# Layer 1's cosine sums: both layer norms of the tokens as one scale, ln_g and ln_b in ScalarE's evictions, a Gram matrix of unscaled queries, unrolled batches

## What is computed

```
x = x + _L1_xattn_ref(_layernorm(x, axis=-1), ctx_1024, ctx_1024, ...)

def layer_norm(x, g, b, eps=1e-05):
    mu = x.mean(-1, keepdims=True)
    var = ((x - mu) ** 2).mean(-1, keepdims=True)
    return (x - mu) / jnp.sqrt(var + eps) * g + b

f_q, f_k, f_v = (proj(q), proj(k), proj(v))      # proj: layer_norm(t, ln_g, ln_b) @ w_in.T
q_centered = f_q - f_q.mean(-1, keepdims=True)
feat_corr = jnp.einsum('hnd,hne->hde', q_flat, q_flat) / q_flat.shape[1]
q_global = f_q.mean(axis=(1, 2))
k_global = f_k.mean(axis=(1, 2))
```

## Time and profile before

| | |
|---|---|
| runs | 4522.26, 4522.98, 4527.35 us; median 4522.98 us |
| profiled execution | span 4527.3 us (to the page's rounding, the run of 4527.35 us) |
| mean granted TensorE clock | 0.907 |
| busy, whole span | TensorE 86%, VectorE 68%, ScalarE 45%, GpSimd 18% |
| `cosine_sums` | 1171.8 to 1323.7 us of the span |

### The profile page before, as it was taken

How to read it: one execution, slowest core, us unless ns; L and a number is a source line. 1 busy time by engine, 2 the same in 40 slices (tenths; PEclk the granted TensorE clock), 3 DMA queues, 4 the chain that set the end, 5 groups by cost and what they waited for, 6 DMA issues and landing times. The chain is left out here.

```text
span 4527.3 us, 83053 instructions
## 1 busy us (share of the span) xinstructions
PE 3886.3 (86%) x30431; PEld 2824.0 (62%) x30525; DVE 3074.1 (68%) x7110; ACT 2057.9 (45%) x3636; POOL 795.1 (18%) x510
## 2 busy tenths in 40 slices
PE   6799997799377999796399999779997987999899
PEld 5344443798365777575378888635555665555577
DVE  7666664456746666544566666678867887888587
ACT  3355554233103333342044444347775762777510
POOL 6433321401431000000023322410000013000000
PEclk9799999599668999897599999879998998999999
DMA  8233331201311000011054544722210015222000
GB/s 266 86 100 101 101 91 54 68 26 42 125 62 33 19 19 19 28 40 37 13 158 124 132 125 125 230 80 66 66 38 19 1 35 199 60 67 67 28 19 19
DMA packets 234478, 338.02 MB, mean 75 GB/s; under 512 B 39204, under 2 KB 132950, under 8 KB 234167
## 3 DMA queue, kind: packets, MB, share of 16 engines
q1 hardware_dynamic: 218280, 306.66, 21.4%
q0 software_dynamic: 15888, 27.23, 2.8%
HBM read 242.42 MB, written 107.01 MB: 77 GB/s over the span
## 5 line engine op out<-in xcount | busy, mean ns | idle before, releaser
L1918 ACT ACTIVATE a_pT<-a_psS 128x512 f32<-128x512 f32 x1536 | 836.0, 597 | 387.7 <-PE a_psS L1804 382.4
L1990 DVE TENSOR_REDUCE a_mx<-a_psA 128x1 f32<-128x512 f32 x1024 | 656.4, 685 | 82.9 <-PE a_psA L1782 82.8
L1819 PE MATMUL a_psZ<-a_pT,a_V 128*17 128x128 f32 x12288 | 488.8, 278 | 0.0
L1782 PE MATMUL a_psA<-a_ks,a_qs 48*128 48x512 f32 (+1 forms) x1536 | 405.5, 523 | 83.8 <-DVE a_mx L1990 36.9
L1986 DVE CUSTOM_DVE_ANT_0 a_scored<-a_psA,a_hide_q 128x512 bf16<-128x512 f32 x512 | 332.7, 688 | 184.4 <-PE a_psA L1782 183.3
L1819 PEld LDWEIGHTS a_psZ<-a_pT,a_V 128*17 128x17 f32 x12288 | 272.8, 97 | 272.7 <-issue 163.3
L1782 PEld LDWEIGHTS a_psA<-a_ks,a_qs 48*128 48x128 f32 (+1 forms) x1536 | 151.6, 192 | 330.2 <-DVE a_mx L1990 127.7
L1804 PE MATMUL a_psS<-a_qs,a_ks 50*128 50x512 f32 (+1 forms) x1536 | 318.3, 408 | 2.7 <-ACT a_pT L1918 0.8
L3262 DVE SCALAR_TENSOR_TENSOR ex_h<-ex_psU,ex_ub,ex_sg 128x512 f32<-128x512 f32 x129 | 96.9, 751 | 189.3 <-PE ex_psU L159 182.3
L2002 POOL TENSOR_TENSOR X<-X,a_osb 128x512 f32<-128x512 f32 x48 | 61.1, 1278 | 935.3 <-ACT a_osb L1905 917.3
L3208 ACT CAST ex_w_h<-X 128x1024 fp32r<-128x1024 f32 x102 | 106.0, 1040 | 149.5 <-DMA X<-in_L_ffn_gw 145.7
(11 more groups left out here) (606 smaller groups left out, 10227.2 us busy)
## 6 DMA issues: line engine op xcount, KB each, us to landing
a_qs<-a_q_parts SPq DMA_DIRECT2D x576, 64.0 KB, 2.3
a_ks<-a_k_parts SPq DMA_DIRECT2D x576, 64.0 KB, 2.3
a_k_parts<-a_p_kp SPq DMA_DIRECT2D x96, 256.0 KB, 2.6
a_q_parts<-a_p_qp SPq DMA_DIRECT2D x96, 256.0 KB, 3.2
X<-in_L_ffn_gw SPq DMA_DIRECT2D x36, 512.0 KB, 4.4
X<-in_L_ffn_up_w SPq DMA_DIRECT2D x36, 512.0 KB, 3.3
X<-in_L_ffn_down_w SPq DMA_DIRECT2D x36, 512.0 KB, 3.8
top_rows<-blank_rows SPq DMA_DIRECT2D x32, 514.0 KB, 4.8
```

Source lines behind the costliest of these rows:

```text
L1782: nc.tensor.matmul(psA[:, unit(a, par) % 3], qs[r, g % ring, p % 2, q * P:(q + 1) * P], ks[r, g % ring, p % 2], start=True, stop=True).the ...
L1819: last = nc.tensor.matmul(psZ[q * VP:q * VP + VW, g % 2, j * P:(j + 1) * P], V[:, b, kt, g % NG * GH + j, :], pT[:, p % 2, par, kt, q * P: ...
L1918: nc.scalar.activation(pT[:, p % 2, par, kt, :], psS[:, unit(t, par) % 3], ACT.Exp).then_inc(exp_done, 1)
L1990: nc.vector.tensor_reduce(mx[:, p // 2 % 2, par, p % 2, q:q + 1], psA[:, unit(a, par) % 3], AX_X, ALU.max).then_inc(a_used, 1)
```

## The change

Only `cosine_sums` is changed. The two norms of the tokens become one scale and one shift per token, worked out from the moments of `x` alone: the scale is the reciprocal root of `var * (1 + eps) + eps * eps`. ScalarE applies them to the tokens (`normalise`), VectorE normalises the context. Neither is multiplied by `ln_g` at that point. TensorE transposes the unscaled operands; ScalarE's eviction (`take`) applies `ln_g` and `ln_b`, now one per partition, and sums each row as it goes. The Gram matrix is that of the unscaled queries, upper blocks only; behind the last batch VectorE and TensorE put together the Gram matrix of the scaled ones from it, the sums and `ln_g`, `ln_b`. GpSimd only sets two constants. Batches are unrolled instead of looped, `zT`, `var`, `std`, `rstd` get two buffers. ScalarE's root of batch b+1 stands ahead of its work on batch b; VectorE's moments of batch b+1 stand ahead of the scales of batch b; the take of the queries of batch b-1 stands behind the normalisation of batch b. On SyncE the load of batch b+2 stands ahead of the two stores of batch b.

The added lines, with their surroundings (the lines taken out are those of the kernel before, printed above):

```diff
 def cosine_sums(nc, A, G, z_dram, gsum, later_loads, later_loaded):
...
     with ExitStack() as ctx:
         sb = lambda n, s, d=F32: ctx.enter_context(nc.sbuf_tensor("l1s_" + n, s, d))
         psum = lambda n, s, d=F32: ctx.enter_context(nc.psum_tensor("l1s_" + n, s, d))
         sem = ctx.enter_context(stage_semaphores(nc, "l1s_"))
         cx = sb("cx", [P, 2, TB, D])
...
+        stats, meanvar = sb("stats", [P, 2, TB, 6]), sb("meanvar", [P, 2, 2, TB, 2])
+        var, std, rstd, shift = (sb(n, [P, 2, 2, TB]) for n in ("var", "std", "rstd", "shift"))
+        norm = sb("norm", [P, 2, 2, TB, D])
+        lng, lnb = sb("lng", [P, D]), sb("lnb", [P, D])
+        g_col, b_col = sb("g_col", [P, KD]), sb("b_col", [P, KD])
+        zeros, ones = sb("zeros", [P, P]), sb("ones", [P, P])
+        zT = sb("zT", [P, 2, 2, KD, S])
+        part_sums, zsum = sb("part_sums", [P, 2, KD, B]), sb("zsum", [P, 2, KD])
+        scaled, diag, row = sb("scaled", [P, KD]), sb("diag", [P, KD, P]), sb("row", [P, D])
+        gram = sb("gram", [P, KD, D])
         psT = psum("psT", [P, 2, KD, S])
...
+        psG, psR = psum("psG", [P, KD, S]), psum("psR", [P, S])
         loaded, set_up = sem("loaded"), sem("set_up")
         cx_loaded = [sem("cx_loaded0"), sem("cx_loaded1")]
...
+        z_of = lambda n, b: z_dram[1 - n].rearrange("(k p) t -> p k t", p=P)[:, :, b * S:(b + 1) * S]
 
         with nc.Block() as block:
             @block.sync
             def _(sp):
...
+                def load(b):
+                    sp.dma_start(cx[:, b % 2], ctx_rows[b]).then_inc(cx_loaded[b % 2], 16)
+
+                load(0)
+                for tile, src in ((g_col, "L1_xattn_ln_g"), (b_col, "L1_xattn_ln_b")):
+                    sp.dma_start(tile[:], A[src].rearrange("(k p) -> p k", p=P), allow_slow_non_contiguous=True).then_inc(loaded, 16)
+                load(1)
                 for tile, src in ((lng, "L1_xattn_ln_g"), (lnb, "L1_xattn_ln_b")):
                     sp.dma_start(tile[:], bcast_row(A[src])).then_inc(loaded, 16)
                 for tile, src in later_loads:
                     sp.dma_start(tile, src).then_inc(later_loaded, 16)
...
+                for b in range(B):
+                    if b + 2 < B:
+                        sp.wait_ge(k_ready, b + 1)
+                        load(b + 2)
+                    for n in (K_, Q_):
+                        sp.wait_ge(zT_ready[n], KD * (b + 1))
+                        sp.dma_start(z_of(n, b), zT[:, n, b % 2]).then_inc(z_stored[n][b % 2], 16)
                 for n in range(2):
...
+                    for s in range(2):
+                        sp.wait_ge(z_stored[n][s], 16 * B // 2)
+                sp.wait_ge(loaded, 64)
                 sp.wait_ge(later_loaded, 16 * len(later_loads))
+
+            @block.gpsimd
+            def _(pool):
+                nc.gpsimd.memset(zeros[:], 0.0).then_inc(set_up, 1)
+                nc.gpsimd.memset(ones[:], 1.0).then_inc(set_up, 1)
 
             @block.tensor
             def _(pe):
+                def turn(n, b):
+                    pe.wait_ge((q_ready, k_ready)[n], b + 1)
+                    if b > 0:
+                        pe.wait_ge(zT_ready[n], KD * b)
+                    for t in range(TB):
+                        for k in range(KD):
+                            last = nc.tensor.transpose(psT[:, n, k, t * P:(t + 1) * P], norm[:, n, b % 2, t, k * P:(k + 1) * P], G.ident[:])
+                    last.then_inc(zT_in_psum[n], 1)
+
+                pe.wait_ge(set_up, 2)
                 for m in range(KD):
                     nc.tensor.matmul(psG[:, m, 0:P], zeros[:], zeros[:], start=True, stop=False, skip_group_check=True)
...
+                for b in range(B):
+                    turn(K_, b)
+                    turn(Q_, b)
+                    for m in range(KD):
                         for t in range(TB):
...
+                            last = nc.tensor.matmul(psG[:, m, m * P:D], norm[:, Q_, b % 2, t, m * P:(m + 1) * P], norm[:, Q_, b % 2, t, m * P:D],
+                                                    start=False, stop=(b == B - 1 and t == TB - 1), skip_group_check=True)
+                    last.then_inc(gram_done, 1)
+
+                pe.wait_ge(diag_ready, KD)
+                for m in range(KD):
+                    last = nc.tensor.matmul(psR[:, m * P:(m + 1) * P], ones[:], diag[:, m], start=True, stop=True)
+                last.then_inc(row_in_psum, 1)
+                pe.wait_ge(upper_ready, 1)
+                nc.tensor.transpose(psR[:, D:D + P], gram[:, 0, P:D], G.ident[:]).then_inc(lower_in_psum, 1)
 
             @block.scalar
             def _(act):
...
+                def roots(b):
+                    act.wait_ge(var_ready, b + 1)
+                    nc.scalar.activation(std[:, b % 2], var[:, b % 2], ACT.Sqrt).then_inc(std_ready, 1)
+
+                def normalise(b):
+                    act.wait_ge(shift_ready, b + 1)
+                    if b >= 2:
+                        act.wait_ge(gram_done, b - 1)
+                    for t in range(TB):
+                        last = nc.scalar.activation(norm[:, Q_, b % 2, t, :], G.X[:, b * TB + t, :], ACT.Identity,
+                                                    scale=rstd[:, b % 2, Q_, t:t + 1], bias=shift[:, b % 2, Q_, t:t + 1])
+                    last.then_inc(q_ready, 1)
+
+                def take(n, b):
+                    act.wait_ge(zT_in_psum[n], b + 1)
+                    if b >= 2:
+                        act.wait_ge(z_stored[n][b % 2], 16 * (b // 2))
+                    for k in range(KD):
+                        nc.scalar.activation(zT[:, n, b % 2, k, :], psT[:, n, k, :], ACT.Identity, scale=g_col[:, k:k + 1],
+                                             bias=b_col[:, k:k + 1], accum_out=part_sums[:, n, k, b:b + 1]).then_inc(zT_ready[n], 1)
+
+                roots(0)
+                act.wait_ge(loaded, 64)
+                for b in range(B):
+                    if b + 1 < B:
+                        roots(b + 1)
+                    normalise(b)
+                    if b > 0:
+                        take(Q_, b - 1)
+                    take(K_, b)
+                take(Q_, B - 1)
 
             @block.vector
             def _(dve):
...
+                link = chained(dve, chain)
+
+                def moments(b):
+                    dve.wait_ge(cx_loaded[b % 2], 16 * (b // 2 + 1))
+                    if b > 0:
+                        dve.wait_ge(aggr_done, b)
+                    for t in range(TB):
+                        nc.vector.bn_stats(stats[:, Q_, t, :], G.X[:, b * TB + t, :])
+                    for t in range(TB):
+                        last = nc.vector.bn_stats(stats[:, K_, t, :], cx[:, b % 2, t, :])
+                    last.then_inc(stats_done, 1)
+                    dve.wait_ge(stats_done, b + 1)
+                    for n in range(2):
                         for t in range(TB):
...
+                            last = nc.vector.bn_aggr(meanvar[:, b % 2, n, t, :], stats[:, n, t, :])
+                    last.then_inc(aggr_done, 1)
+                    dve.wait_ge(aggr_done, b + 1)
+
+                    nc.vector.tensor_scalar(var[:, b % 2, Q_], meanvar[:, b % 2, Q_, :, 1], 1.0 + LN_EPS, LN_EPS * LN_EPS, ALU.mult, ALU.add)
+                    nc.vector.tensor_scalar(var[:, b % 2, K_], meanvar[:, b % 2, K_, :, 1], LN_EPS, None, ALU.add).then_inc(var_ready, 1)
+
+                def scales(b):
+                    dve.wait_ge(std_ready, b + 1)
+                    nc.vector.reciprocal(rstd[:, b % 2], std[:, b % 2]).then_inc(rstd_ready, 1)
+                    dve.wait_ge(rstd_ready, b + 1)
+                    nc.vector.scalar_tensor_tensor(shift[:, b % 2], meanvar[:, b % 2, :, :, 0], -1.0, rstd[:, b % 2], ALU.mult, ALU.mult
+                                                   ).then_inc(shift_ready, 1)
+                    if b >= 2:
+                        dve.wait_ge(zT_in_psum[K_], b - 1)
                     for t in range(TB):
...
+                        last = nc.vector.tensor_scalar(norm[:, K_, b % 2, t, :], cx[:, b % 2, t, :], meanvar[:, b % 2, K_, t, 0:1],
+                                                       rstd[:, b % 2, K_, t:t + 1], ALU.subtract, ALU.mult)
+                    last.then_inc(k_ready, 1)
+
+                moments(0)
+                for b in range(B):
+                    if b + 1 < B:
+                        moments(b + 1)
+                    scales(b)
+
+                dve.wait_ge(zT_ready[Q_], KD * B)
+                link(nc.vector.tensor_reduce(zsum[:], part_sums[:], AX_X, ALU.add))
+                for m in range(KD):
+                    nc.vector.tensor_scalar(diag[:, m], G.ident[:], zsum[:, Q_, m:m + 1], None, ALU.mult).then_inc(diag_ready, 1)
+                link(nc.vector.scalar_tensor_tensor(scaled[:], b_col[:], -float(N_TOK), zsum[:, Q_], ALU.mult, ALU.add))
+                for n in range(2):
```

(55 more changed lines are left out.)

92 lines of the change are left out of this document (removed).

## The result

The kernel before took 4525.16 us (median of 4 runs, 4522.26 to 4536.67), the changed one 4476.12 us (4 runs, 4471.42 to 4487.62): a ratio of 0.989, 95% interval 0.9873 to 0.9907, or 49.0 us less (42 to 57 by the interval). Forecast were 43.3 us less, 4480 us, and a batch of 13.0 us.

The account below looks back on a forecast made before the run. A chain, no full engine, bounds the stage; a new ring of 4.1 + 3.87 + 0.5 + 3.87 + 0.7 = 13.0 us a batch replaces 16.94, saving 43.3 us: 4522.98 - 43.3 = 4479.7, range 4467 to 4497.

Parts of the forecast that it names:

- The old ring: Before the change: ScalarE's root, VectorE's normalisations, GpSimd, TensorE's transposes, ScalarE's copy, next root; 16.94 us a batch.
- the ring through SyncE's order: On SyncE each context load stands behind the previous batch's store of Q, one load per ring: 13.0 us a batch.
- (a): Landing of the 512 KB context load: 4.1 us, with the store of Q issued just ahead before and after alike.
- (b): VectorE's moments, from the load's landing to the end of the variances, now two operations: 3.87 us.
- (c): VectorE's reciprocal 0.20 us, an equally small scalar_tensor_tensor, and three hand-overs of 0.03 to 0.04: 0.5 us.
- (d)+(e): ScalarE's four normalise operations, 2.1 us, and take of Q, 1.46 for the pair plus row sums at 0.2 each: 3.87.
- (f): SyncE, from the end of ScalarE's take to the next load's issue: 0.7 us, ends 0.65 and 1.2.
- the rival of the growing landing: The load's landing grows between two 512 KB stores; gain gone at 11.3 us, 4533 us in all at 13; 2%.
- the rival of the function tables: ScalarE reloads tables between root and Identity, 1.28 us each: 4488 us; 9%, including other ScalarE costs up to 4500.
- The tail: Stage end after batch 6's shift: last takes, TensorE's last products, assembly of about 5 us; +20.9 us, ending at 1280.4.
- What was costed at nothing: Loads of g and b before ScalarE's first normalise, 2 us if their cover fails; unrolling, bounds -1 and +5.
- The load hidden: Rival: SyncE runs ahead, engines set the batch at 6.5 to 10.5 us instead of 13.0; 4441 to 4465 us; 5%.

## Why the prediction was right, and where it was not

**The bound and the ring.** Right. The old ring is open and the ring through SyncE's order stands in its place: the run with the load moved ahead of the store took it away, the third buffer spread it over two batches, and the statistics moved out of it shortened it by their own length. The start of the stage to the shift of batch 6 took 87.7 us, as forecast, though partly by luck: the start up to the shift of batch 1 was 0.7 us shorter and the five rings behind it 0.8 longer (66.0 against 65.2).

**The terms.** The sum of 13.0 came out at 13.1, but its terms were off by up to 1.0 us, and the landing's excess of 1.0 is cancelled by 0.9 from the other four. That the sum is so close is luck. Measured from the ring shown above:

```
term                                        forecast  measured
(a) landing of the load                          4.1      5.08
(b) moments, to the second variance             3.87      3.66
(c) reciprocal, shift, hand-overs               0.5       0.34
(d)+(e) normalise and take(Q)                   3.87      3.59
(f) end of take to the next load's issue        0.7       0.44
sum                                            13.04     13.11
```

The step that failed is the sentence in (a), "The store of Q is issued just ahead of it before and after alike". Before, the load came 0.67 to 0.99 us behind that store, with nothing behind it for over 9 us; after, it comes 0.41 behind one store and has another 1.1 us behind itself. The prediction looked at the order of the queue but not at the distances, and it did not ask what follows the load. By its own words, landings well above 4.1 would show it wrong; here they did so for this term alone. The DMA list of the stage, in the columns of the earlier trace rows, gives the median:

```profile
l1s_cx<-in_ctx SPq DMA_DIRECT2D x8, 512.0 KB, 4.9
```

This is the rival of the growing landing in small: one microsecond of its break-even of seven, some 6 us of the gain. The Trainium skill ("DMA: Bandwidth & Descriptors", Queues, rings and completion order) has each DMA engine take the descriptors of a ring in their order, while a later write may finish before an earlier one. A store ahead on the same queue would by that delay the load, and one behind may take time from it too. The runs agree: 4.4 us with a store of Q just ahead against 3.7 with none, and 5.1 with the store of K behind as well.

**(f), the gap on SyncE.** The low end of the range, 0.65, was still too high. The prediction kept the whole 0.59 from the copy's end to the end of the store's issue. That held 0.22 us ahead of the store's start (1214.61 in the trace of before), which probably was the loop's address work too: in unrolled code the store of Q starts 0.03 us after the take's end, and the load 0.41 after that.

**(d) and (e), ScalarE.** The unit costs built from far rows were close. The groups by form of the stage, in the columns of the earlier trace rows:

```profile
L2198 ACT ACTIVATE l1s_zT<-l1s_psT,l1s_b_col,l1s_g_col 128x512 f32<-128x512 f32 x32 | 24.3, 767 | 2.0 <-PE l1s_psT L2156 2.0
L2189 ACT ACTIVATE l1s_norm<-X,l1s_shift,l1s_rstd 128x256 f32<-128x256 f32 x32 | 16.6, 590 | 0.6
L2198 ACT ACTIVATION_READ_ACCUMULATOR l1s_zT<-l1s_psT,l1s_b_col,l1s_g_col 128x1 f32 x32 | 6.3, 196 | 0.0
```

The forecast had 0.77, 0.60 and, by analogy with VectorE, an own instruction of 0.2 for the sum along the row. All three held. What it missed is that the read overlaps both neighbours: the second ACTIVATE of the take starts 0.76 after the first, where without a read the overlap seen elsewhere would have made that 0.67. It adds 0.09, and at the end of the chain again 0.09, from the end of the ACTIVATE to its own end: 0.18 for the pair where the forecast had 0.4. There is no table load in the stage, so the rival of the function tables had no part.

The forecast set the rule that multiplications and additions belong on VectorE beside this, at 5 us. The run with the queries on VectorE took 4.4 us from the stage: of the 1.3 us a batch that its loop lost, the normalisation explains 0.7 and shorter landings most of the rest, and the ends gave back 2.0. The Trainium skill ("ScalarE: Activation LUTs", Rules for kernel authors) has multiplications and additions on VectorE, and the trace agrees for fp32, with 1.38 against 2.07 us.

**The tail.** Forecast 20.9 us behind the shift of batch 6, measured 18.0 (1262.82 to 1280.79). VectorE's timeline of the assembly, which answers to the earlier trace rows:

```profile
1275.36 0.18 DVE L2255 TENSOR_REDUCE l1s_zsum<-l1s_part_sums 128x4 f32<-128x32 f32 x1 [9.64 <-ACT l1s_zT L2198]
...
1278.07 0.88 DVE L2271 SCALAR_TENSOR_TENSOR l1s_gram<-l1s_gram,l1s_g_col,l1s_lng 128x256 f32<-128x256 f32 x2
...
1279.91 0.88 DVE L2277 SCALAR_TENSOR_TENSOR l_gsum<-l1s_row,l1s_b_col,l1s_gram 128x256 f32<-128x256 f32 x2
```

The assembly takes 5.4 us, about as forecast. The rest was shorter: the takes last 1.5 and not 1.8, and the last eight Gram products 2.78, below the 3.3 of the estimate:

```profile
1272.85 2.78 PE L2167 MATMUL l1s_psG<-l1s_norm 128*128 128x256 f32 x16
```

That is 2.9 us of the stage: forecast 108.6, measured 105.7. As the stretch ahead of the tail came out as forecast, the tail alone makes 46.2 us of gain in the stage out of the 43.3.

**What was costed at nothing.** The rows of ln_b landed at 1185.95, 8.3 us after their issue. ScalarE's wait for them stands ahead of its second root, whose input was ready at 1186.21: the cover held, by 0.3 us. In the two kernels with the tokens' statistics first it did not. With that edit alone the input was ready at 1180.67, and the root ran at 1181.64:

```profile
1181.64 0.21 ACT L2182 ACTIVATE l1s_std<-l1s_var 128x8 f32<-128x8 f32 x1 [4.47 <-DMA l1s_lnb<-in_L_xattn_ln_b]
```

Nothing in the trace prices the unrolling.

**The load hidden.** Not so here; but its price was wrong as well. The prediction would have had 6.5 to 10.5 us a batch with the load out of the ring; with it out, a batch takes 5.2. ScalarE's 5.9 counted the reads as 0.2 each, VectorE's 5.8 was above the 5.10 measured, and TensorE's 10.5 assumed the lower clock, while in that kernel the granted clock was 1.00, which is 2.4 GHz.

## What to carry to other kernels

When a chain is opened, follow the queue that issues the loads in its written order: a wait for a store ahead of a load puts the store's whole ancestry in front of the load, and two buffers then hide nothing. Either of two cheap edits shows it, the load ahead of the store (13.1 to 9.0 us a batch) or one more buffer (about 6.8, three rings of 20.5 us), and together they reach the engines' own time (5.2). Read a transfer's time with its neighbours: how far ahead the last one on its queue was issued, and how far behind the next.

## What the runs showed of the hardware

A 512 KB load lands in 3.64 to 3.88 us when the nearest store on its queue is 5 us ahead or more and 2.3 us behind, in 4.33 to 4.53 with a 512 KB store 0.41 us ahead, and in 4.89 to 5.72 with another 1.1 us behind as well (three runs). The single packets in the traces, 1024 bytes each of the load and 2048 of the stores, show two different effects. The load's first packet starts 1.05 to 1.18 us after its issue with no store near, and 1.94 to 2.13 us with one 0.41 us ahead, when all but 5 to 12 of that store's 256 packets have started (the run with K stored later): the load waits behind the store. Its last packet ends 3.96 to 4.19 us after its issue in that run, and 4.56 to 5.04 in the change, where 50 to 200 packets of the store of K start before that end: the two run in the same stretch. What a second queue would make of it was not tried. Other loads count as well: the loop's first load in the change, with no store ahead, took 5.05 us, and the last weight load of 1 MB ahead of it landed only 2.3 us after its issue.

The granted clock of TensorE, a mean over its two levels of 1.2 and 2.4 GHz, is 0.76 in the change's 13 us rings, with 5.9 us of TensorE's work in the one shown and 7.1 us idle. In the 9.0 us rings of the load moved ahead it is 1.00, with 4.8 us of work and 4.2 idle; the busy time by stretch, in the columns of the earlier trace rows:

```profile
1201.50:1210.50 9.00, 4.78 (x32) 4.17 (x32) 5.20 (x25) 5.38 (x14) 0.00 (x0) 1.00 0.48 175
```

The shorter ring thus went with the higher clock, and TensorE's own work was shorter as well.

VectorE's tensor_scalar from SBUF stood still for 1.65 us beside GpSimd's addition, and of its group only the one operation that ran into it did; the other three took 0.40 each. The Trainium skill ("SBUF — State Buffer", SBUF: two separate sides) describes this as an exclusive hold on a port pair for a whole instruction, and the trace agrees: the operation ended 0.15 us after the addition. A second operation of each batch met the addition for the queries, on VectorE and GpSimd of before:

```profile
1209.92 1.43 DVE L2221 TENSOR_SCALAR l1s_var<-l1s_meanvar 128x8 f32<-128x8 f32 x1
```

```profile
1208.98 2.34 POOL L2196 TENSOR_TENSOR l1s_zq<-l1s_zq,l1s_lnb 128x1024 f32<-128x1024 f32 x1
```

This variance took 1.43 us in place of the 0.17 of the earlier trace rows and ended 0.03 us after the addition. It cost nothing, as ScalarE's root stood behind a copy until 1214.28. The statistics beside GpSimd's multiplication took their usual 1.39 us (1206.39, GpSimd from 1206.55), so not every VectorE operation is held.
